# Where the constants load, when the fills go out, and five steps in another order

## The chip, the core and the metric

The kernel runs on one core of a Trainium2 chip. The metric is the device time of one execution in microseconds; lower is better. Before the change the median of three timed runs is 674.17 us (673.79 to 674.68). The core's engines are TensorE (PE; its weight loads are listed as PEld), VectorE (DVE), ScalarE (ACT), GpSimd (POOL) and SyncE (SP, which here only issues DMAs). Each engine runs its own list of instructions in order and waits on semaphores for the others. DMAs are issued by SP, ACT and POOL and are carried out by 16 DMA engines that all queues share.

## The reference

The input is 4096 tokens of 128 values. The six steps of a "macaron" block follow one another, each with a layer norm ahead of it and a residual around it:

```python
x = x + 0.5 * ffn0(norm(x))   # 8 experts 128->512->128, gelu, each token to its argmax expert
x = x + attn0(norm(x))        # grouped causal conv (4 taps), pooled q/k by cumulative sums, gelu MLP
x = x + 0.5 * ffn0(norm(x))   # the same weights as the first
x = x + 0.5 * ffn1(norm(x))   # 16 experts, capacity 320 rows each, relu, softmax gate
x = x + attn1(norm(x))        # s = a*s + W_b u along time, W_c, layer norm
x = x + 0.5 * ffn1(norm(x))   # the same weights as the fourth
```

In `ffn0` every token is computed by one expert out of 8. In `ffn1` a token that comes after the first 320 of its expert is left as it is. All values are float32.

## The kernel before, in words

The tokens lie as 32 tiles of 128 rows in the on-chip array `X`, handled as 8 chunks of four tiles. The stages follow each other: expert pass 0 (`ffn0`), attention, expert pass 1 (`ffn0` again), the first MoE stage (`ffn1`), recurrence, the second MoE stage.

**Expert passes.** A router scores the chunks (`pturn`, `pcopy`, `pscore`), picks the expert (`plog`, `oh`), ranks the tokens (`ra`, `rrank`, `rb`) and computes a row index for each token (`rsel`). POOL then sends each tile of 128 rows to its places in a DRAM table `xs0` with an indirect DMA (`send`, L1620). This is done in groups: pass 0 has two groups of 3 and 5 chunks, pass 1 three groups. The table is then worked through in 84 tiles of one expert each: tiles 0 to 40 belong to pass 0, 41 to 83 to pass 1. For tile i, SP loads its rows (`tload`, L696) and its expert's first weights, 256 KB (`tw`, L703, a ring of four buffers, so a load waits for `tup` of tile i-4); DVE adds the second bias to a copy (`txb`, L1242) and normalises (`tn`, L1233); PE transposes (`tturn`, L817), DVE copies (`tx`, L1247), PE multiplies (`tup`, L827), ACT applies gelu (`tgelu`, L1513), PE multiplies again (`tdown`, L835), DVE joins the residual (`ty`, L1253) and POOL sends the rows back to a DRAM array `y` (`home`, L1624). SP reads `y` back into `X` (`yload`, L711). `txb` reads the row array `RW` after ACT has scaled a part of it (`hb2`, L1484).

**MoE stages.** The second router works by chunk: PE transposes and scores (`pturn`, `pscore` L784), DVE picks an expert (`q1`, seven operations, L1200 to L1214), PE ranks (`qrank`, L809 to L811), DVE makes the row index (`q3`, L1220 and L1227), POOL sends the four tiles (`send`) into a table `xs1` with a place for 320 rows for each of 16 experts. For expert i SP loads rows (`eload`, L730) and weights, 512 KB (`wload`, L722, seven buffers); PE runs `eturn`, `eup` (L900), `edown` (L907), `eback` (L914); DVE makes `eout` (L1387), POOL sends home (L1624).

**Fills.** The tables must hold a neutral row wherever no token is sent. `fill0` writes the places of one group of `xs0` from a zero tile (`ZB`, L633 and L636). `fill1` writes the 320 rows of four experts of `xs1` from `ZX` (four DMAs of 185 KB, L650). The fills of pass 1's three groups are the steps fill.0 to fill.2 of SP's list, those of the first MoE stage's table fill.3 to fill.6, those of the second's fill.7 to fill.10. `FILL_AFTER` (L89) says which semaphore each waits for: `aout` n means that attention chunk n has ended, `edown` n that expert n has.

**Bulk constants.** ACT issues, as its step bulk.1 (L1465 and L1466), two DMAs: the rest of `RW` (256 KB) and all matrices of the attention and recurrence, `MT` (1096 KB), and the semaphore `cm` counts them. Readers are cen.1 on PE (L764), whose result ACT copies in cenc.1; wc.0 on DVE (L998 to L1004); and the attention.

**Recurrence.** For each chunk DVE takes statistics (`rstat`, L1397 and L1401), ACT a square root (`rstd`, L1579), DVE a reciprocal (`rinv`, L1406), ACT normalises (`rnorm`, L1591). ACT's list begins rstd.0, rstd.1, rnorm.0, rnorm.1.

**Order.** The order of all steps on each engine is written out by hand in `TABLE`, one list for each engine; `ORDER` splits it, and the engine programs walk it. A step that waits holds up everything behind it in its own list. Among PE's steps are fillers: `heat` (L920) and `warm` (L932), matmuls of constants into a free bank, whose results nobody reads; each is held back by a semaphore named in `HEAT` or `WARM`. `issued` there counts POOL's sends in the MoE stages.

Of the kernel before, what the change touches and what calls it, by code (L numbers as in the profile page):

```python
# [193 lines left out]
eload.11 eload.12 wload.12 wload.13 wload.14 eload.13 eload.14 eload.15 fill.7 fill.8 wload.15 wload.16 wload.17 fill.9 wload.18 fill.10 yload.16
yload.17 yload.18 yload.19 yload.20 yload.21 yload.22 wload.19 store.0 yload.23 wload.20 wload.21 wload.22 eload.16 eload.17 eload.18 eload.19
eload.20 eload.21 store.1 store.2 store.3 store.4 store.5 store.6 store.7 wload.23 wload.24 eload.22 eload.23 eload.24 wload.25 wload.26 eload.25
eload.26 wload.27 wload.28 eload.27 eload.28 wload.29 eload.29 eload.30 eload.31 wload.30 wload.31""",
# [6 lines left out]
tturn.23 tup.21 tup.22 tturn.24 tdown.20 tdown.21 tdown.22 tturn.25 tup.23 tturn.26 tup.24 tup.25 tdown.23 tdown.24 tup.26 tturn.27 tdown.25 tturn.28
tup.27 tdown.26 tturn.29 tup.28 aturn1.0 aturn1.1 tturn.30 tup.29 tdown.27 aconv.0 tturn.31 tdown.28 tdown.29 aconv.1 tturn.32 tup.30 tturn.33 tup.31
aturn2.0 tup.32 tdown.30 tturn.34 tdown.31 aq.0 tdown.32 tturn.35 ak.0 aturn2.1 tup.33 tup.34 aq.1 av.0 tdown.33 tturn.36 tup.35 ak.1 tup.36 tdown.34
tdown.35 tturn.37 aturn3.0 av.1 tturn.38 tup.37 tup.38 tturn.39 tdown.36 tdown.37 tdown.38 tturn.40 tup.39 aturn3.1 tup.40 aturn4.0 tdown.39 tdown.40
# [4 lines left out]
ak.7 pturn.8 pturn.9 pscore.11 pscore.12 av.7 aup.24 aup.25 aup.26 aturn3.7 aup.27 rrank.3 adown.5 adown.6 aturn4.7 pturn.10 pturn.11 aup.28 aup.29
aup.30 tturn.41 aup.31 tturn.42 tup.41 tturn.43 adown.7 pscore.13 pscore.14 tturn.44 pturn.12 tup.42 tturn.45 tdown.41 tup.43 tturn.46 pscore.15
tup.44 tdown.42 tturn.47 tdown.43 tdown.44 rrank.4 tup.45 tup.46 tup.47 tturn.48 tdown.45 tdown.46 tdown.47 tturn.49 tturn.50 tup.48 tturn.51 tup.49
tup.50 tdown.48 tdown.49 tturn.52 tdown.50 tup.51 tturn.53 tup.52 tup.53 tturn.54 tdown.51 tdown.52 tdown.53 tturn.55 tup.54 tturn.56 tup.55 tup.56
tturn.57 tdown.54 tdown.55 tturn.58 tdown.56 tturn.59 tup.57 tup.58 tturn.60 tturn.61 tup.59 tdown.57 tdown.58 tdown.59 tturn.62 tup.60 tup.61 tup.62
tdown.60 tturn.63 tdown.61 tup.63 tturn.64 tdown.62 tturn.65 tup.64 tdown.63 tturn.66 tup.65 tdown.64 tturn.67 tup.66 tturn.68 tdown.65 tup.67
tdown.66 tturn.69 tup.68 tdown.67 tturn.70 tup.69 tturn.71 tdown.68 tturn.72 tup.70 tup.71 tturn.73 tdown.69 tdown.70 tdown.71 tturn.74 tup.72 tup.73
tup.74 tturn.75 tdown.72 tdown.73 tturn.76 tup.75 tup.76 tturn.77 tdown.74 tdown.75 pturn.13 tturn.78 tup.77 tdown.76 pscore.16 tup.78 tdown.77
qrank.0 tturn.79 pturn.14 pturn.15 tturn.80 pscore.17 tdown.78 tup.79 tup.80 tturn.81 qrank.1 pturn.16 pscore.18 pscore.19 tup.81 tdown.79 tdown.80  # L220
tdown.81 tturn.82 qrank.2 tturn.83 tup.82 tup.83 pturn.17 tdown.82 tdown.83 pscore.20 qrank.3 qrank.4 warm.0 pturn.18 pturn.19 pscore.21 pturn.20
pscore.22 warm.1 warm.2 pscore.23 qrank.5 warm.3 warm.4 qrank.6 qrank.7 warm.5 warm.6 warm.7 warm.8 warm.9 warm.10 warm.11 warm.12 warm.13 warm.14
warm.15 warm.16 warm.17 warm.18 warm.19 warm.20 warm.21 warm.22 warm.23 warm.24 warm.25 warm.26 warm.27 warm.28 eturn.0 eup.0 eup.1 eturn.1 eup.2
# [1535 lines left out]
```

How the kernel before makes its waits and increments, by code:

```python
    def wait_ge(self, sem, value):  # L388
        if self.passed.get(sem.name, 0) < value:
            self.passed[sem.name] = value
            self.eng.wait_ge(sem, value)
# [160 lines left out]
        def wait_r(lane, b):  # L552
            lane.wait_ge(*((sem("pinv"), b + 1) if b < NBS else (sem("ppow"), b - NBS + 1)))
# [32 lines left out]
        def wait_x(lane, k):  # L587
            p, c = divmod(k, NC)
            if p == 0:
                lane.wait_ge(sem(f"y{c}"), 16)
            elif p == 1:
                lane.wait_ge(sem("aout"), c + 1)
            elif p == 2:
                wait_y(lane, NC + c)
            else:
                lane.wait_ge(sem("rout"), c + 1)
# [1 line left out]
        def wait_y(lane, j):  # L598
            lane.wait_ge(sem(f"y{j % NC}"), turns(j + NC, NC))
# [8 lines left out]
        def wait_home(lane, t):  # L609
            lane.wait_ge(sem(f"home{t % NHS}"), turns(t, NHS))
# [6 lines left out]
        def wait_table(lane, g, i):  # L617
            if not IS_LAST[g] or i >= E0:
                lane.wait_ge(sem("rte"), 3 * (g + 1))
# [1 line left out]
        def wait_scattered(lane, g):  # L622
            k = g - GP.index(GP[g])
            lane.wait_ge(sem(f"sent{k}"), 16 * sum(GNT[j] for j in range(g + 1) if j - GP.index(GP[j]) == k))
# [20 lines left out]
        def fill1(e, m, a):  # L645
            SP.wait_ge(sem("zero"), 5)
            for q in range(4 * a, 4 * a + 4):
                dst = xs1[m][q * REACH:q * REACH + CAP, :].rearrange("(p r) d -> p r d", r=5)
                e.dma_start(dst, ZX[0:CAP // 5, :].unsqueeze(1).broadcast_to([CAP // 5, 5, ROWX])).then_inc(sem("fillx"), 16)
```

## Time and profile before

| | |
|---|---|
| timed runs | 674.17 us median, 673.79 to 674.68 |
| profiled execution | 672.23 us, of which 670.8 us from the first instruction to the last |
| mean granted TensorE clock | 0.949 of full speed |
| busy share | PE 92%, DVE 67%, POOL 55%, ACT 48% |
| DMA | 94.19 MB, mean 140 GB/s |
| stages, us from the start | router 0 to 43, expert pass 0 to about 153, attention to 271, expert pass 1 (beginning inside it) to 369, router to 411, first MoE stage to 504, recurrence to 557, second MoE stage to the end |

A row of the timeline gives the start, the duration, the engine, the line and operation, the tiles written and read, and in brackets how long the engine stood idle before it and what ended that wait. The chain of waits is followed back from the last instruction: at each step to what released it. Waits of an engine that is off that chain cost nothing by themselves.

### The profile page before, as it was taken

The numbers are of one execution on the slowest core, as the hardware profiler recorded it, in microseconds if no ns is written. First come the engines' busy times: TensorE is split into PE (matmuls) and PEld (weight loads), VectorE is DVE, ScalarE is ACT, GpSimd is POOL, SyncE is SP. The second block draws the span as 40 slices with busy tenths as digits, with TensorE's granted clock in tenths as the row PEclk, the third lists the DMA queues.
The fourth block names the chain that finished last, engine by engine and source line by source line (L and its number), as shares of the span: only waits on it lengthen the run. The fifth ranks groups of instructions, "written<-read, shape, count | busy, mean of one in ns | idle before, by whom it ended". The sixth has DMA issues, their size and how long they took to land.

```text
span 670.8 us, 13130 instructions
## 1 busy us (share of the span) xinstructions
...
## 2 busy tenths in 40 slices
...
GB/s 266 311 212 194 187 213 202 105 49 201 54 0 83 10 91 61 267 211 201 211 272 99 178 68 104 81 151 141 133 217 142 148 56 51 154 132 142 99 104 15
DMA packets 87031, 94.19 MB, mean 140 GB/s; under 512 B 12156, under 2 KB 65439, under 8 KB 86704
## 3 DMA queue, kind: packets, MB, share of 16 engines
...
q14 instruction: 40, 0.33, 0.2%
...
## 4 chain that ended last, share of the span: by engine, by line
PE 63%; DVE 10%; DMA 8%; POOL 6%; issue 5%; ACT 3%; SPq 3%; ACTq 0%; DVEq 0%
PE ps L835 10%; PE ps L827 10%; PE ps L907 6%; PE ps L900 6%; PE ps L882 4%; PE ps L932 4%; PE ps L784 4%; PE ps L745 4%; POOL y L1624 3%; PE ps L849 3%; PE ps L875 3%; POOL xs L1620 2%; PE ps L945 2%; PE ps L817 2%; DMA X<-y 1%
## 5 line engine op out<-in xcount | busy, mean ns | idle before, releaser
L1620 POOL DMA_INDIRECT xs<-X,IDX x128 | 125.8, 982 | 102.9 <-issue 64.1
L1513 ACT ACTIVATE ht<-ps,CL 128x128 f32<-128x128 f32 x336 | 93.0, 379 | 84.6 <-PE ps L827 84.4
L1624 POOL DMA_INDIRECT y<-yt,xi x84 | 83.1, 989 | 48.9 <-DVE yt L1253 33.5
L827 PE MATMUL ps<-xt,w1s 128*128 128x128 f32 x672 | 86.3, 277 | 1.8 <-DVE xt L1247 0.8
L835 PE MATMUL ps<-W,ht 128*128 (+1 forms) x672 | 85.0, 277 | 2.1 <-ACT ht L1513 1.9
L835 PEld LDWEIGHTS ps<-W,ht 128*128 128x128 f32 x672 | 80.0, 192 | 4.4 <-issue 4.2
L827 PEld LDWEIGHTS ps<-xt,w1s 128*128 128x128 f32 x672 | 80.0, 192 | 3.8 <-DVE xt L1247 2.4
L1611 POOL TENSOR_TENSOR sma<-sma,MH 128x4 f32<-128x4 f32 (+1 forms) x24 | 30.6, 1278 | 71.4 <-DVE sma L962 65.1
L932 PE MATMUL ps<-MT,KC 128*128 128x512 f32 x118 | 58.2, 648 | 1.6 <-DVE IDX L1227 1.2
L1570 ACT ACTIVATE hb<-ps 128x320 f32<-128x320 f32 x64 | 26.7, 428 | 51.1 <-PE ps L900 50.8
L1563 ACT ACTIVATE w1s<-x,SE 128x128 f32<-128x128 f32 (+1 forms) x66 | 27.4, 483 | 43.7 <-DVE SE L1356 43.6
L1611 POOL TENSOR_TENSOR SE<-SE,MH 128x3 f32<-128x3 f32 x32 | 27.9, 873 | 33.7 <-DVE SE L1352 33.5
L1253 DVE SCALAR_TENSOR_TENSOR yt<-ps,xb 128x128 f32<-128x128 f32 x84 | 24.0, 286 | 33.2 <-PE ps L835 32.6
L932 PEld LDWEIGHTS ps<-MT,KC 128*128 128x128 f32 x118 | 23.6, 208 | 29.7 <-issue 21.3
L1624 POOL DMA_INDIRECT y<-xu,x x36 | 34.7, 963 | 16.8 <-DVE xu L1387 8.5
L900 PE MATMUL ps<-ht,W 128*128 128x320 f32 x136 | 41.7, 435 | 0.0
L900 PE MATMUL ps<-ht,wx 128*128 128x320 f32 x120 | 37.3, 436 | 3.4 <-DMA wx<-in_w1x 1.8
L907 PE MATMUL ps<-hb,W 128*128 128x320 f32 x136 | 39.7, 436 | 0.4 <-DVE hb L1374 0.3
L1247 DVE COPY xt<-ps 128x128 f32<-128x128 f32 x84 | 24.2, 288 | 22.1 <-PE ps L817 21.6
L1495 ACT ACTIVATE pxt<-ps 128x512 f32<-128x512 f32 x29 | 16.8, 596 | 40.5 <-PE ps L745 40.3
L1374 DVE TENSOR_SCALAR hb<-ps 128x320 f32<-128x320 f32 x64 | 30.5, 484 | 8.5 <-PE ps L900 8.0
L907 PE MATMUL ps<-hb,wx 128*128 128x320 f32 x120 | 35.1, 435 | 0.4 <-DVE hb L1374 0.3
...
## 6 DMA issues: line engine op xcount, KB each, us to landing
w1s<-in_w SPq DMA_DIRECT2D x84, 256.0 KB
...
X<-y SPq DMA_DIRECT2D x24, 256.0 KB, 4.7
...
```

What stands on the lines that cost most here:

```text
L745: r = e.transpose(dst[:, j * P:(j + 1) * P], src[:, j, 0:P], ident)
L827: r = e.matmul(ps[TILE_BANKS[i % n]][:, c * P:(c + 1) * P], W1[i % NW1][:, c * P:(c + 1) * P], XTT[i % NX][:, :], start=True, stop=True)
L835: r = e.matmul(ps[TILE_BANKS[i % len(TILE_BANKS)]][:, 0:P], HT[i % NHT][:, c, :], W02[:, bass.ds(r0 * F + c * P, P)], start=(c == 0), stop ...
L900: e.matmul(ps[2 + c][:, 0:CAP], WE[k % NW][:, c * P:(c + 1) * P], XET[k % NXET], start=True, stop=True).then_inc(sem("eup"), 1)
L907: r = e.matmul(ps[6 + i % 2][:, 0:CAP], WE[i % NW][:, F + c * P:F + (c + 1) * P], HB[i % 2][:, c, 0:CAP], start=(c == 0), stop=(c == 3))
L932: e.matmul(b[:, F - w:F], ident, MT[:, 0:w], start=True, stop=True)
L1374: e.tensor_scalar(HB[k % 2][:, c, 0:CAP], ps[2 + c][:, 0:CAP], 0.0, None, ALU.max).then_inc(sem("erelv"), 1)
L1513: r = e.activation(HT[i % NHT][:, c, :], ps[TILE_BANKS[i % len(TILE_BANKS)]][:, c * P:(c + 1) * P], ACT.Gelu, bias=CL[:, bass.ds(r0 * 4 + ...
L1563: r = e.activation(EN[i % NEN][0:n, b, :], xe[0:n, b, 0:P], ACT.Identity, scale=se(i, 27)[0:n, b:b + 1], bias=se(i, 30)[0:n, b:b + 1])
L1611: return e.tensor_tensor(dst, src, MH[:, 0:dst.shape[1]], ALU.pow)
L1620: return e.indirect_dma_start(dst, bass.IndirectOffsetOnAxis(ap=IDX[:, n:n + 1], axis=0), X[:, n, 0:w], None, bounds_check=hi, oob_is_err= ...
L1624: return e.indirect_dma_start(dst, bass.IndirectOffsetOnAxis(ap=ix, axis=0), src, None, bounds_check=hi_home, oob_is_err=False, engine_sem ...
```

## The change

Five things are changed. (1) bulk.1 leaves its place ahead of hb2.0 in ACT's list and stands behind tgelu.3, the gelu of the fourth tile; cen.1 (PE), cenc.1 (ACT) and wc.0 (DVE), which need its data, move back too. (2) `FILL_AFTER` is changed: the three fills of pass 1 wait for the first attention chunk, the eight expert fills for the second (four) and the third (four); in SP's list all eleven stand in a row ahead of tw.41, where fill.5 stood one step and fill.6 seven loads further on, and fill.7 to fill.10 behind the last expert load (eload.15) of the first MoE stage. (3) On DVE tn.0 stands ahead of txb.0, q3.5 ahead of q1.7, and rinv.0 ahead of rstat.1. (4) The fillers warm.1 and warm.2 are no longer in PE's list. (5) Nothing else: all instructions but the two fillers are the same. The lists are written here as pieces, since the lines of the table are broken anew:

```diff
-FILL_AFTER = [("aout", 1 + n // 2) for n in range(len(FILL_GROUPS))] + [("aout", n) for n in (3, 3, 4, 4)] + [("edown", n) for n in (2, 4, 6, 8)]
+FILL_AFTER = [("aout", 1) for n in FILL_GROUPS] + [("aout", n) for n in (2, 2, 2, 2, 3, 3, 3, 3)]
 sp:
-fill.3 fill.4 tw.41 fill.5 tload.41
+fill.3 fill.4 fill.5 fill.6 fill.7 fill.8 fill.9 fill.10 tw.41 tload.41
...
-tw.46 tw.47 fill.6 tload.52
+tw.46 tw.47 tload.52
...
-eload.14 eload.15 fill.7 fill.8 wload.15 wload.16 wload.17 fill.9 wload.18 fill.10 yload.16
+eload.14 eload.15 wload.15 wload.16 wload.17 wload.18 yload.16
 pe:
-tdown.6 tdown.7 cen.1 tturn.9
+tdown.6 tdown.7 tturn.9
...
-tup.15 tdown.14 tturn.17
+tup.15 tdown.14 cen.1 tturn.17
...
-pscore.22 warm.1 warm.2 pscore.23 qrank.5 warm.3 warm.4 qrank.6 qrank.7
+pscore.22 pscore.23 qrank.5 warm.3 warm.4 qrank.6 qrank.7
 dve:
-rb.1 rsel.1 txb.0 tn.0 tn.1
+rb.1 rsel.1 tn.0 txb.0 tn.1
...
-txb.9 tn.10 wc.0 ty.6
+txb.9 tn.10 ty.6
...
-tx.17 txb.17 tx.18
+tx.17 txb.17 wc.0 tx.18
...
-q1.5 q1.6 q1.7 q3.5 q3.6 q3.7
+q1.5 q1.6 q3.5 q1.7 q3.6 q3.7
...
-rstat.0 rstat.1 rinv.0 rstat.2
+rstat.0 rinv.0 rstat.1 rstat.2
 act:
-pstd.2 table.1 bulk.1 hb2.0 tgelu.0 tgelu.1 tgelu.2 tgelu.3 tgelu.4
+pstd.2 table.1 hb2.0 tgelu.0 tgelu.1 tgelu.2 tgelu.3 bulk.1 tgelu.4
...
-tgelu.12 cenc.1 tgelu.13
+tgelu.12 tgelu.13
...
-tgelu.17 tgelu.18 tgelu.19
+tgelu.17 tgelu.18 cenc.1 tgelu.19
```

## Rows read from the trace of the kernel before

**Rows 1.** The page's chain of waits, shares of the span by engine.

```profile
PE 63%; DVE 10%; DMA 8%; POOL 6%; issue 5%; ACT 3%; SPq 3%; ACTq 0%; DVEq 0%
```

**Rows 2.** Table by stage: stretch, length, busy time (instructions) per engine, PEclk, DMA share, GB/s.

```profile
44.00:52.00 8.00, 4.76 (x36) 4.26 (x37) 3.26 (x14) 3.31 (x12) 5.82 (x7) 1.00 1.04 366
52.00:60.00 8.00, 6.57 (x54) 6.04 (x55) 2.87 (x11) 2.83 (x11) 6.17 (x7) 1.00 0.46 138
270.00:300.00 30.00, 28.82 (x257) 28.28 (x256) 21.38 (x99) 13.72 (x49) 21.15 (x22) 1.00 0.82 236
366.00:388.00 22.00, 16.78 (x77) 11.70 (x77) 9.56 (x43) 2.98 (x8) 14.76 (x16) 0.69 0.48 150
```

**Rows 3.** Timeline of the first tiles: start, duration, engine, line, operation, [idle before <-releaser].

```profile
43.58 0.33 PE L817 MATMUL ps<-KC,xh 128*128 128x128 f32 x1 [0.45 <-DVE xh L1233]
50.19 0.29 DVE L1242 TENSOR_TENSOR xb<-xi,RW 128x128 f32<-128x128 f32 x1 [3.07 <-DMA xi<-xs]
51.87 1.13 PE L827 MATMUL ps<-xt,w1s 128*128 128x128 f32 x8 [0.55 <-DMA w1s<-in_w]
```

**Rows 4.** Timeline of SP's DMA issues in expert pass 0.

```profile
45.24 1.47 SPq L703 DMA_DIRECT2D w1s<-in_w  x2
59.18 1.16 SPq L696 DMA_DIRECT2D xi<-xs  x2
69.89 0.33 SPq L696 DMA_DIRECT2D xi<-xs  x1
```

**Rows 5.** DMA issues by line: queue, count, KB each, median us to landing.

```profile
X<-y SPq DMA_DIRECT2D x24, 256.0 KB, 4.7
MT<-in_mats ACTq DMA_DIRECT2D x1, 1096.0 KB, 9.0
```

**Rows 6.** Tile loads (xi) from 30 to 110 us, their landing.

```profile
DMA to landing us min/median/max: 2.6/3.2/7.8
```

**Rows 7.** Timeline of DVE in expert pass 0, tiles 10 and 12.

```profile
64.21 0.36 DVE L1233 TENSOR_SCALAR xh<-xi 128x128 f32<-128x128 f32 x1
74.82 0.34 DVE L1233 TENSOR_SCALAR xh<-xi 128x128 f32<-128x128 f32 x1
```

**Rows 8.** Timeline of ACT: the gelu of the fifth tile.

```profile
58.33 1.91 ACT L1513 ACTIVATE ht<-ps,CL 128x128 f32<-128x128 f32 x7 [4.03 <-PE ps L827]
```

**Rows 9.** Timeline of the first dispatch, 381 to 389 us.

```profile
381.23 3.55 PE L932 MATMUL ps<-MT,KC 128*128 128x512 f32 x4
384.62 0.96 PE L784 MATMUL ps<-MBG,pxt 128*128 128x16 f32 x8
388.03 0.97 POOL L1620 DMA_INDIRECT xs<-X,IDX  x1 [2.65 <-DVE IDX L1227]
```

**Rows 10.** Timeline of the end of the first MoE stage, 475 to 500 us.

```profile
475.30 7.64 SPq L650 DMA_DIRECT2D xs<-ZX  x8
482.98 1.69 SPq L722 DMA_DIRECT2D wx<-in_w1x  x2
489.18 0.81 PE L900 MATMUL ps<-ht,wx 128*128 128x320 f32 x2 [1.81 <-DMA wx<-in_w1x]
499.20 0.97 POOL L1624 DMA_INDIRECT y<-xu,x  x1 [0.33 <-DVE xu L1387]
```

**Rows 11.** Timeline of the start of the recurrence.

```profile
508.36 0.84 DVE L1397 BATCH_NORM_STATS2 sma<-X 128x6 f32<-128x128 f32 x4
508.48 0.30 ACT L1579 ACTIVATE sma<-sma,EP 128x4 f32<-128x4 f32 x1 [13.15 <-DVE sma L1401]
509.85 2.60 ACT L1591 ACTIVATE hn<-X,sma 128x128 f32<-128x128 f32 x8
```

**Rows 12.** Timeline of SP between attention and expert pass 1: fills, first weight load.

```profile
208.82 7.51 SPq L650 DMA_DIRECT2D xs<-ZX  x8
238.63 0.36 SPq L703 DMA_DIRECT2D w1s<-in_w  x1
```

**Rows 13.** Table by stage, the stretch of those fills.

```profile
208.80:216.40 7.60, 7.60 (x55) 6.32 (x54) 7.36 (x18) 3.69 (x7) 0.00 (x0) 1.00 0.70 145
```

More of the change, by code:

```diff
@@ L194 @@
[L194 to L197, printed above, removed]
+tw.36 tw.37 tw.38 tw.39 tw.40 yload.3 yload.4 yload.5 yload.6 yload.7 fill.0 fill.1 fill.2 fill.3 fill.4 fill.5 fill.6 fill.7 fill.8 fill.9 fill.10
@@ L204 @@
[L204 to L207, printed above, removed]
@@ L212 @@
[L212 to L215, printed above, removed]
@@ L216 @@
[L216 to L223, printed above, removed]
@@ L240 @@
-edown.31 eback.31""",
+tup.15 tdown.14 cen.1 tturn.17 tup.16 tturn.18 tup.17 tturn.19 tdown.15 tturn.20 tdown.16 tup.18 tup.19 tdown.17 tdown.18 tturn.21 tdown.19 tturn.22
+tup.20 tturn.23 tup.21 tup.22 tturn.24 tdown.20 tdown.21 tdown.22 tturn.25 tup.23 tturn.26 tup.24 tup.25 tdown.23 tdown.24 tup.26 tturn.27 tdown.25
+tturn.28 tup.27 tdown.26 tturn.29 tup.28 aturn1.0 aturn1.1 tturn.30 tup.29 tdown.27 aconv.0 tturn.31 tdown.28 tdown.29 aconv.1 tturn.32 tup.30
+tturn.33 tup.31 aturn2.0 tup.32 tdown.30 tturn.34 tdown.31 aq.0 tdown.32 tturn.35 ak.0 aturn2.1 tup.33 tup.34 aq.1 av.0 tdown.33 tturn.36 tup.35 ak.1
@@ new lines @@
+pscore.8 pscore.9 pscore.10 ak.6 av.6 adown.3 aturn4.4 aturn4.5 aturn3.6 aup.16 aup.17 aup.18 rrank.2 aup.19 aturn2.7 adown.4 aq.7 aup.20 aup.21
+aup.22 aup.23 aturn4.6 ak.7 pturn.8 pturn.9 pscore.11 pscore.12 av.7 aup.24 aup.25 aup.26 aturn3.7 aup.27 rrank.3 adown.5 adown.6 aturn4.7 pturn.10
+pturn.11 aup.28 aup.29 aup.30 tturn.41 aup.31 tturn.42 tup.41 tturn.43 adown.7 pscore.13 pscore.14 tturn.44 pturn.12 tup.42 tturn.45 tdown.41 tup.43
+tturn.46 pscore.15 tup.44 tdown.42 tturn.47 tdown.43 tdown.44 rrank.4 tup.45 tup.46 tup.47 tturn.48 tdown.45 tdown.46 tdown.47 tturn.49 tturn.50
@@ new lines @@
+tdown.71 tturn.74 tup.72 tup.73 tup.74 tturn.75 tdown.72 tdown.73 tturn.76 tup.75 tup.76 tturn.77 tdown.74 tdown.75 pturn.13 tturn.78 tup.77 tdown.76
+pscore.16 tup.78 tdown.77 qrank.0 tturn.79 pturn.14 pturn.15 tturn.80 pscore.17 tdown.78 tup.79 tup.80 tturn.81 qrank.1 pturn.16 pscore.18 pscore.19
+tup.81 tdown.79 tdown.80 tdown.81 tturn.82 qrank.2 tturn.83 tup.82 tup.83 pturn.17 tdown.82 tdown.83 pscore.20 qrank.3 qrank.4 warm.0 pturn.18
+pturn.19 pscore.21 pturn.20 pscore.22 pscore.23 qrank.5 warm.3 warm.4 qrank.6 qrank.7 warm.5 warm.6 warm.7 warm.8 warm.9 warm.10 warm.11 warm.12
@@ L241 @@
+eup.118 eup.119 eback.27 eturn.30 edown.28 eup.120 eup.121 eturn.31 eback.28 edown.29 eup.122 eup.123 eback.29 eup.124 edown.30 eup.125 eup.126
+eup.127 eback.30 edown.31 eback.31""",
     "dve": """
 pstat.0 pstat.1 pstat.2 pinv.0 plog.0 oh.0 pnm.0 ra.0 rb.0 rsel.0 pstat.3 pstat.4 pstat.5 pstat.6 pinv.1 pstat.7 plog.1 pinv.2 plog.2 pnm.1 oh.1 oh.2
[L243 removed]
```

80 lines of the change are left out of this document (43 added, 37 removed).

## The prediction

> **What bounds the kernel now.** I read four views. First the chain of waits [rows 1]: TensorE carries 63% of what ends last, DVE 10%, DMA 8%, POOL 6%. So a microsecond counts only where TensorE stands still for something, or where the sends on POOL are the chain. Second, the table by stage [rows 2] shows where that is: from 44 to 52 us TensorE is busy 4.76 of 8 us while the DMA engines are full (share 1.04); from 366 to 388 it is busy 16.78 of 22 us at a mean granted clock of 0.69. In the attention it has nearly nothing to give. Third, the timeline of each such place, for the instruction that is waited for. Fourth, SyncE's timeline, for what stands ahead of the load that came late. A stage that is bound by TensorE hands a gain made before it on to the stages behind, so the gains add.
>
> **Start of the first expert pass.** Two things hold it.
> First tile: the normalisation tn.0 stands behind txb.0, which waits for ACT's scaling of RW (hb2), and that behind the issue of the bulk constants. Both go. But the fillers on TensorE last until the first transposition: only 0.45 us of idle time stands before it [rows 3], so 0.45 is all this gives.
> Fourth tile: DVE stands 3.07 us until 50.19 for a tile load and TensorE starts tup.3 only at 51.87, on weights that SP issued at 45.24 [rows 3, 4]. In that stretch the constants, 1096 + 256 KB, are on the same engines; the larger takes 9.0 us to land [rows 5]. Without them I take for this 256 KB load the 4.7 us of the other 256 KB loads that SP issues [rows 5]: 49.94, and 0.1 to the matmul, 50.03 instead of 51.87, or 1.85 us. Bounds: 0.45 if it lands as late as now; 2.65 if TensorE's own order is what is left (tup.2 and the transposition before it, 0.45 earlier: about 49.2).
> What is late next: the load of tile 12, issued at 69.89 [rows 4], waits for the last send of group 1. POOL sends those one behind the other and gains only where the first tile's result, 0.45 us earlier at best, stands in its row. Issue 69.89 plus the median landing of 3.2 [rows 6] is 73.1; DVE normalises the tile at 74.82 [rows 7]. So 1.7 us can pass here, and up to 2.1 with what POOL gains; 1.85 does.
> The constants come back: bulk.1 now stands behind tgelu.3, which ends at 58.33 - 4.03 = 54.30 [rows 8], then 1.85 earlier. The issue itself is hidden in ACT's 4.03 us of waiting for TensorE. The transfer lies beside SP's weight loads and the loads of tiles 10 and 11 (issued at 59.18, then about 57.3). Tile 10 is normalised at 64.21 [rows 7], then 62.4: 5 us after its issue. If it takes the 7.8 us of the slowest tile load [rows 6], it lands at 65.1 and 2.7 us are lost, which turns the whole start into 0.85 later than now. At the median it costs nothing. In 52 to 60 the share is 0.46: at the 366 GB/s seen at 1.04 the free half holds some 1.5 MB, more than the 1.35 MB. I take no cost. Term: -1.85, between -2.1 and +0.85.
> The Trainium skill bears on this: "DMA: Bandwidth & Descriptors" (Queues, rings and completion order) says that each DMA engine takes turns, packet by packet, between the queues that have work. By that the loads on SP's queue would keep half the rate beside ACT's constants and be late by under a microsecond; by the slowest row they are late by 4.6. The trace's 3.07 us stand on tile 3 is nearer to the row. The sum would be the same by the rule and 2.7 us higher by the row.
> cen.1, cenc.1 and wc.0 move back with the constants; the same instructions, and their readers (convolution, recurrence, second router) come tens of microseconds later. Zero.
>
> **The fills.** Pass 1's third fill goes out one chunk earlier, and all 32 issues of the expert fills stand ahead of tw.41, at the end of the second and of the third attention chunk. Eight such issues take 7.51 us of SP from 208.82 on [rows 12], so 16 take 15: the last is out at 224. The next on SP, tw.41, is due at 238.63 [rows 12], because it waits for the router; 14.8 us are spare. The eight of now run with a DMA share of 0.70 while TensorE is busy 7.60 of 7.60 us [rows 13]: no slowing is seen, so zero. What leaves the second expert pass (four issues) gives at most the 1.18 us that TensorE is not busy in 270 to 300 [rows 2]; no wait there names these loads, so I take zero.
> In the first MoE stage it is different. At 475.30 SP issues eight fills for 7.64 us, and only then the weights of expert 15, at 482.98; TensorE stands 1.81 us for them until 489.18 [rows 10]. Without the fills that load goes out at 475.3, twelve us ahead of its need at 487.4. What follows is arithmetic: the last rows go home 0.33 us after POOL's last instruction, released by DVE's result and not by a queue of POOL [rows 10]. Term: -1.8, between 0 and -1.81.
>
> **The first dispatch.** POOL stands 2.65 us until 388.03 for q3.5 [rows 9]; its usual gap is 0.30. Ahead of q3.5 stand the two fillers (3.55 us, at half clock) that hold pscore.23 back until 384.62, and then q1.7 on DVE. Both leave. The score matmuls then run at half the clock, twice 0.96 [rows 9], so of about 3.4 us gained some 0.9 goes back: q3.5 is done 2.5 earlier, at 385.3, and earlier still by what q1.7 took. POOL is free at 388.03 - 2.65 = 385.38 and goes on at 385.68. q3.6 is needed only four sends later. 2.35 us go from the chain of sends, on which the loads of the experts wait. I take -2.2, since the 24 fillers that remain ahead of the experts start at a clock that may still be low; between 0 and -2.35.
>
> **The recurrence.** rinv.0 now stands ahead of rstat.1. Today rstat.1 starts at 508.36 with no wait, and ACT's square root for chunk 0 runs from 508.48 for 0.30 [rows 11]. So DVE will stand until 508.8, and rstat.1 begins about 0.6 later. ACT gains nothing from the early rinv.0: rnorm.0 at 509.85 stands behind rstd.1 [rows 11], which needs rstat.1. DVE is nearly full behind it. Between 0 (chunk 1 lands later than now) and +0.6; I take +0.45.
>
> **Sum.** -1.85 - 1.8 - 2.2 + 0.45 = -5.4 on the profiled execution's 672.23, that is 666.8. The median of the timed runs lies 1.94 above that execution; on its scale 674.17 - 5.4 = 668.8 us.
>
> **Rivals.**
> The constants collide where they are now put. For it: the 7.8 us of the slowest tile load, the same 1.35 MB. Against: the share of 0.46 there, and prefetch eight tiles deep. Start term between 0 and +0.85 instead of -1.85: 670.7 to 671.5.
> The dispatch gain ends in another wait: the experts start on fillers or on their weights. For: TensorE is busy with fillers up to the first expert. Against: the loads wait for the sends. 668.8 + 2.2 = 671.0.
> Slower: the clock. Over the 22 us from 366 the granted clock is 0.69, so 13.6 us at the lower level (1.2 GHz); TensorE had stood still, waiting for loads and indices, before it fell. Two fillers leave just this stretch. If TensorE enters the experts at the lower level for as long a spell, 13.6 us of its work double in length for the half that would have been done: 6.8 us, 668.8 + 6.8 = 675.6. It decides from 10.8 us at that level, where it eats the 5.4. Against: 24 fillers, each waiting only for sends that POOL makes in an unbroken row. The Trainium skill's "TensorE: Matmul & The Clock Gate" (HAM oscillation) says that idle gaps put the engine back to half clock until it has been active again; that is what the 0.69 shows.
> The change does not do what it says: the gains are swallowed, because the stage behind starts on something that did not move (POOL's homes, a late landing). About 673.5. Against: the chain's 63% on TensorE.
>
> **How the numbers follow.** The forecast has 0.60 (own range 667.0 to 670.6, from the bounds of its terms); the colliding constants 0.14; the lost dispatch gain 0.09; the swallowed gains 0.10; the clock 0.07. A measurement of this kernel tells about 0.2% (1.35 us) from no change. Faster by more: 0.60 + 0.14 + 0.09 = 0.83; within: 0.10; slower: 0.07. The range that leaves out 0.2: up to the lost gains and halfway to the swallowed ones, 672.3; down to all terms at their best with 1.2 from the second pass (2.1 + 1.81 + 2.35 + 1.18 less 0 = 7.4), 666.7, and half a microsecond for the runs' own spread: 666.2.
>
> **What would show it.** Right: tup.3 near 50 us, no wait of DVE for the fourth tile load; no fill on SP after 225; POOL's sends of the first dispatch 1.28 apart throughout; the weights of expert 15 issued right behind the last expert load and no wait of TensorE for them; DVE standing some 0.35 us ahead of rinv.0. Wrong: a wait of DVE on tile 10 or 11 near 62 us; a granted clock below 1 after the first expert starts; SP late at tw.41; the second pass starting at the time of now.

## The result, and the profile after

| | before | after |
|---|---|---|
| first comparison, 4 executions each | 674.42 us median (673.79 to 677.89) | 665.14 us median (663.77 to 669.42), ratio 0.9874 [0.9832, 0.9915] |
| all later comparisons together | 670.13 us mean, 670.28 median, standard deviation 2.55, 119 executions | 663.74 us mean, 663.63 median, standard deviation 2.12, 21 executions |
| profiled execution (span) | 672.23 (670.8) | 665.63 (663.6) |

The change makes the kernel faster. The first comparison says 9.3 us, the later ones 6.4 us (standard error 0.5; ratio 0.9905 [0.989, 0.992]). Four executions of the kernel before that fell in its slow state (674.9 to 678.1 us) are left out of the second line. The forecast was a gain of 5.4 and a time of 668.8 (666.2 to 672.3); 665.14 lies 1.1 us below that range.

The page of the kernel after, its chain of waits and its clock in 40 slices:

```profile
PE 57%; DVE 12%; POOL 12%; DMA 8%; issue 8%; ACT 3%; SPq 1%; ACTq 0%; DVEq 0%; POOLq 0%
PEclk8599999999999999999998689999999996999999
```

SPq has fallen from 3% to 1% [rows 1], as it would with the fills gone from ahead of expert 15's weights. POOL has doubled to 12%: where TensorE no longer holds the sends up, POOL's own row is the chain. The table by stage, for the stretches of [rows 2] and for one more, 350 to 360:

```profile
44.00:52.00 8.00, 6.93 (x58) 6.28 (x56) 4.06 (x16) 4.45 (x16) 6.10 (x7) 1.00 0.76 213
52.00:60.00 8.00, 6.83 (x56) 6.54 (x57) 3.23 (x14) 2.43 (x9) 5.94 (x7) 1.00 0.92 311
270.00:300.00 30.00, 29.02 (x258) 28.48 (x258) 20.81 (x94) 15.30 (x56) 21.21 (x22) 1.00 0.73 209
350.00:360.00 10.00, 9.73 (x75) 9.49 (x75) 5.90 (x26) 4.35 (x14) 7.74 (x8) 0.84 0.52 153
366.00:388.00 22.00, 17.75 (x76) 12.55 (x77) 10.51 (x47) 2.17 (x5) 16.13 (x17) 0.61 0.51 157
```

From 44 to 52 TensorE is busy 6.93 us instead of 4.76, and the constants' transfer now stands in 52 to 60 (share 0.92 instead of 0.46). The third row has hardly moved. The fourth has a granted clock of 0.84 although TensorE is busy 9.73 of 10 us; this is what the forecast had no place for.

The steps one by one in the kernel after. The start: the fourth tile's matmuls, the constants' two issues, tile 10, the load of tile 12 and tile 12:

```profile
48.69 1.16 PE L827 MATMUL ps<-xt,w1s 128*128 128x128 f32 x8 [0.39 <-DVE xt L1247]
50.67 0.35 ACTq L1465 DMA_DIRECT2D RW<-in_rows  x1
51.05 0.65 ACTq L1466 DMA_DIRECT2D MT<-in_mats  x1
61.26 0.35 DVE L1233 TENSOR_SCALAR xh<-xi 128x128 f32<-128x128 f32 x1
69.09 0.33 SPq L696 DMA_DIRECT2D xi<-xs  x1
72.57 0.40 DVE L1233 TENSOR_SCALAR xh<-xi 128x128 f32<-128x128 f32 x1 [1.08 <-DMA xi<-xs]
```

The fourth tile starts 3.18 us earlier [rows 3]. Tile 10, beside the constants, starts 2.95 earlier and, in this execution, without a wait [rows 7]. Tile 12's load goes out only 0.80 earlier [rows 4], and there DVE now stands 1.08 us: some of the gain goes back. Tile 12 itself is still normalised 2.25 earlier [rows 7].

Other executions with the constants at their new place do wait at tile 10: DVE stands 1.74 us in b_start, 1.56 in a_wide, 0.99 in a_ring11 and 0.37 in a_rinvback (all runs below). In b_start, DVE and then TensorE:

```profile
63.18 0.35 DVE L1233 TENSOR_SCALAR xh<-xi 128x128 f32<-128x128 f32 x1 [1.74 <-DMA xi<-xs]
64.35 0.30 PE L817 MATMUL ps<-KC,xh 128*128 128x128 f32 x1 [0.86 <-DVE xt L1247]
```

That load was issued at 56.34, 6.84 us before the normalisation; in nine executions with the constants at their old place these are 4.9 to 5.1 us, and DVE does not wait.

The timeline further on: SyncE's fills in the attention and the first load behind them; the first send of chunk 5 in the first dispatch; the last weight loads of the first MoE stage and TensorE's matmuls of its last experts (L900, then L907):

```profile
183.90 40.41 SPq L650 DMA_DIRECT2D xs<-ZX  x18
236.14 0.36 SPq L703 DMA_DIRECT2D w1s<-in_w  x1
384.88 0.97 POOL L1620 DMA_INDIRECT xs<-X,IDX  x1 [0.30 <-issue]
473.66 0.90 SPq L722 DMA_DIRECT2D W<-in_w1x  x2
483.39 1.78 PE L900 MATMUL ps<-ht,wx 128*128 128x320 f32 x6
485.33 2.36 PE L907 MATMUL ps<-hb,wx 128*128 128x320 f32 x8
```

And the table by stage beside the fills:

```profile
207.00:224.00 17.00, 17.00 (x99) 12.16 (x98) 16.33 (x58) 7.35 (x14) 5.22 (x4) 1.00 0.72 149
```

The last fill is out at 224.3 and the weight load behind it, which waits for the router, at 236.14, no later than before [rows 12]. TensorE is busy 17.00 of 17 us at full clock beside them, as beside the eight of before [rows 13]. POOL's stand of 2.65 us is the usual 0.30 [rows 9]. TensorE no longer stands for expert 15: the L900 row at 483.39 has no wait [rows 10].

### The profile page after: what moved, and what is told of

Read it like the earlier page. It is cut to its first block, busy times and chain, and to the rows that moved or that the text cites. A ratio compares the mean times of both kernels' runs of the same rounds, so it can differ in the third digit from the quotient of the medians.

```text
span 663.6 us, 13121 instructions
## 1 busy us (share of the span) xinstructions
PE 612.0 (92%) x3647; PEld 472.9 (71%) x3647; DVE 448.8 (68%) x1882; ACT 323.4 (49%) x1037; POOL 367.2 (55%) x377
## 4 chain that ended last, share of the span: by engine, by line
PE 57%; DVE 12%; POOL 12%; DMA 8%; issue 8%; ACT 3%; SPq 1%; ACTq 0%; DVEq 0%; POOLq 0%
PE ps L907 8%; PE ps L900 8%; PE ps L835 8%; PE ps L827 8%; POOL xs L1620 8%; PE ps L932 4%; PE ps L784 3%; PE ps L882 3%; PE ps L745 3%; PE ps L849 3%; POOL y L1624 2%; PE ps L875 2%; DMA y<-yt,xi 2%; PE ps L890 1%; PE ps L914 1%
## 5 line engine op out<-in xcount | busy, mean ns | idle before, releaser
L827 PE MATMUL ps<-xt,w1s 128*128 128x128 f32 x672 | 86.7, 278 | 1.9 <-DVE xt L1247 1.2
L835 PEld LDWEIGHTS ps<-W,ht 128*128 128x128 f32 x672 | 81.4, 195 | 4.3 <-issue 4.2
L827 PEld LDWEIGHTS ps<-xt,w1s 128*128 128x128 f32 x672 | 80.2, 192 | 4.3 <-DVE xt L1247 2.2
L932 PE MATMUL ps<-MT,KC 128*128 128x512 f32 x114 | 55.8, 646 | 0.4
L1624 POOL DMA_INDIRECT y<-xu,x x36 | 34.7, 964 | 14.7 <-issue 8.3
L900 PE MATMUL ps<-ht,W 128*128 128x320 f32 x136 | 41.7, 435 | 0.0
L907 PE MATMUL ps<-hb,W 128*128 128x320 f32 x136 | 39.7, 436 | 0.4 <-DVE hb L1374 0.3
L900 PE MATMUL ps<-ht,wx 128*128 128x320 f32 x120 | 37.1, 435 | 1.6 <-DVE ht L1368 1.3
L907 PE MATMUL ps<-hb,wx 128*128 128x320 f32 x120 | 35.1, 436 | 0.4 <-DVE hb L1374 0.3
```

The lines of the kernel that those rows point to most:

```text
L827: r = e.matmul(ps[TILE_BANKS[i % n]][:, c * P:(c + 1) * P], W1[i % NW1][:, c * P:(c + 1) * P], XTT[i % NX][:, :], start=True, stop=True)
L835: r = e.matmul(ps[TILE_BANKS[i % len(TILE_BANKS)]][:, 0:P], HT[i % NHT][:, c, :], W02[:, bass.ds(r0 * F + c * P, P)], start=(c == 0), stop ...
L900: e.matmul(ps[2 + c][:, 0:CAP], WE[k % NW][:, c * P:(c + 1) * P], XET[k % NXET], start=True, stop=True).then_inc(sem("eup"), 1)
L907: r = e.matmul(ps[6 + i % 2][:, 0:CAP], WE[i % NW][:, F + c * P:F + (c + 1) * P], HB[i % 2][:, c, 0:CAP], start=(c == 0), stop=(c == 3))
L932: e.matmul(b[:, F - w:F], ident, MT[:, 0:w], start=True, stop=True)
L1624: return e.indirect_dma_start(dst, bass.IndirectOffsetOnAxis(ap=ix, axis=0), src, None, bounds_check=hi_home, oob_is_err=False, engine_sem ...
```

## The experiments

Fifteen runs, in the order of the questions. "At equal clock" means: the times of 244 executions of eleven kernels were fitted with one level for each kernel and one slope on the mean granted clock; the slope is -0.40 us (+-0.03) for each 0.001, and levels have a standard error of about 0.55.

### Is 9.3 us the change?

b_same, the kernel before, and a_same and a_again, the kernel after; nothing is edited:

```diff
 (no line differs)
```

> The kernel before, unchanged, once more. Theory A (single spells at the lower clock level come and go between executions of one and the same kernel): the spells that its first profile showed at 224.0 to 227.4 us and at 541.5 to 544.9 us are not both there again, others may stand elsewhere, and the times of its executions differ by 0.66 us for each 0.001 of their mean granted clock. Theory B (each spell belongs to the order of the instructions): the same spells at the same places within 1 us, and the executions agree in clock to 0.001. Time: ratio 1.000 in both.

> The changed kernel, unchanged, once more. Theory A: its single spell at 356.8 to 360.2 us is gone or elsewhere, a spell near 220 or near 537 may be there as in the kernel before, and executions between 663 and 669 us follow their mean granted clock by 0.66 us for each 0.001. Theory B: the same spells again, clock 0.957 in each. Time: ratio 0.987 (0.985 to 0.990) in both.

> The changed kernel again, as the base for the next three and for more executions. Theory A (the change is worth 5.5 to 6.5 us; the 9.3 us of the first comparison hold 3 to 4 us of low spells of the clock that its few executions of the kernel before happened to have): ratio 0.990 to 0.992. Theory B (the change is worth 9.3): ratio 0.986 to 0.987.

Measured: b_same 671.49 us median (664.97 to 675.66), ratio 1.0016 [0.9983, 1.0049]; a_same 661.81 (660.85 to 666.96), 0.9904 [0.9869, 0.9938]; a_again 663.75 (660.80 to 667.80), 0.9912 [0.9884, 0.9939]. One and the same kernel spreads over 10 us. Between 40 and 660 us the clock records show the lower level (1.2 GHz) in these stretches:

```
first execution before: 224.0-227.4  370.8-384.4  387.9-391.3  541.5-544.9  551.7-568.8
b_same                : 368.2-381.8  385.2-388.7  487.6-491.1  538.8-545.7  552.5-569.6
first execution after : 356.8-360.2  370.5-387.5  551.4-561.6
a_same                : 355.7-359.1  369.4-386.5  543.5-560.5
a_again               : 366.8-383.9  547.7-557.9
```

The table by stage, 220 to 230 us, of the kernel before in its first execution and then in b_same:

```profile
220.00:230.00 10.00, 10.00 (x62) 8.20 (x61) 8.64 (x26) 4.52 (x11) 4.21 (x3) 0.83 0.00 1
```

```profile
220.00:230.00 10.00, 10.00 (x72) 8.38 (x72) 9.51 (x28) 5.61 (x14) 3.73 (x3) 1.00 0.00 1
```

Of the same kernel, 62 matmuls are through in one and 72 in the other. Theory A holds: single spells come and go with the execution. So the comparison of the two profiles cannot be read as the change alone: the 1.7 us that the attention seemed to win, the 1.7 us that pass 1 seemed to lose at 357 and the 2.7 us that the second dispatch seemed to win are such spells. The slope came out lower than the 0.66 expected, as it would if part of the low time costs nothing (a_wide below has such a stretch). The 6.4 us lie inside the first comparison's interval (5.7 to 11.3); why its four executions of the kernel before stand 5.0 us above the mean of the later 119 stays open. The later comparisons ran on four chips, where the kernel before has means of 669.2, 669.9, 670.9 and 671.0 us; on which chip the first one ran is not on record, so a difference between chips is not ruled out. The Trainium skill, "TensorE: Matmul & The Clock Gate" (Part 1: The HAM clock gate), says that the moment of the change does not follow the kernel's start and so differs from run to run; the rows above agree. The same page of the Trainium skill puts the ramp at the start of the matmuls at under 1% of a typical span; the spells here lie far behind the start, and executions of one kernel span 1.6% (664.62 to 675.24).

### The four parts, one at a time on the kernel before

b_start and b_disp:

```diff
-act: table.1 bulk.1 hb2.0 ... tgelu.3 tgelu.4
+act: table.1 hb2.0 ... tgelu.3 bulk.1 tgelu.4
-dve: rsel.1 txb.0 tn.0
+dve: rsel.1 tn.0 txb.0
...
-pe: pscore.22 warm.1 warm.2 pscore.23
+pe: pscore.22 pscore.23
-dve: q1.6 q1.7 q3.5
+dve: q1.6 q3.5 q1.7
```

(the first two edits, with cen.1, cenc.1 and wc.0 as in the change, are b_start; the last two are b_disp)

> Only the first part of the change: bulk constants behind the gelu of the fourth tile with their readers further back, normalisation of the first tile ahead of its bias copy. Theory of the trace after (3.1 us won at the fourth tile and 2.1 given back because later tile loads wait for buffers that POOL's row of sends and homes frees): the fourth tile's up matmuls at 48.7 us, gain 0.9 to 1.0 at 110 us, time 673.4 or ratio 0.9986, apart from spells of the clock. My forecast's theory (the gain at tile four stays): gain 1.85, ratio 0.9973. Rival (the start also causes the gains in the attention and the second dispatch): ratio 0.993 or less.

> Only the first dispatch: index of chunk 5 ahead of the pick of chunk 7, two fillers out. Theory of both traces: the 2.65 us that POOL stood before the sends of chunk 5 fall to 0.3, all later sends 2.35 us earlier, and the first expert 2.3 to 2.8 earlier; time 671.9, ratio 0.9965, apart from spells. Rival (gain lost at the experts' start): ratio 1.000, first expert not earlier than 1 us.

b_fills and b_rinv:

```diff
-FILL_AFTER = ... [("aout", 1 + n // 2) ...] + [("aout", n) for n in (3, 3, 4, 4)] + [("edown", n) for n in (2, 4, 6, 8)]
+FILL_AFTER = ... [("aout", 1) ...] + [("aout", n) for n in (2, 2, 2, 2, 3, 3, 3, 3)]
...
-dve: rstat.0 rstat.1 rinv.0 rstat.2
+dve: rstat.0 rinv.0 rstat.1 rstat.2
```

> Only the fills of both expert tables moved into the attention. Theory of the traces: the weights of expert 15 are issued right behind the last expert load, TensorE's 1.81 us of standing before 489 go, and with them the low spell of the clock that followed that stand in one execution of the kernel before (487.6 to 491.1, another 1.7 us in the executions that have it): gain 1.8 to 2.6, ratio 0.9961 to 0.9973; nothing lost in the attention, SP on time at tw.41. Rival (16 fills in a row slow the attention): chunk 3 or 4 of the attention later by 1 us or more, ratio 0.999 or above. Rival (the fills explain all that the other parts leave of the change's gain of 5.5): gain 3 or more, ratio 0.9955 or less.

> Only the reciprocal of the recurrence's chunk 0 ahead of the statistics of chunk 1. My forecast: chunk 1's statistics 0.5 to 0.6 later, 0.3 to 0.45 lost, ratio 1.0005, which the times cannot tell from 1. Rival (it is this that brings the 2.6 us won in the second dispatch): ratio 0.996, and both spells of low clock at 541 and from 552 to 569 shorter.

| part | ratio | against the kernel before | at equal clock | by stage in the traces |
|---|---|---|---|---|
| b_start | 1.0019 [0.9982, 1.0056] | -0.1 +-0.9 | -1.0 | -0.8 |
| b_disp | 1.0002 [0.9967, 1.0036] | -1.0 +-0.8 | -2.2 | -2.5 |
| b_fills | 0.9977 [0.9952, 1.0001] | -1.9 +-0.6 | -3.1 | -3.0 |
| b_rinv | 1.0007 [0.9979, 1.0036] | +0.6 +-0.8 | +0.3 | +0.2 |
| sum | | -2.4 | -6.0 | -6.0 |
| whole change | 0.9905 | -6.4 +-0.5 | -6.0 | |

No part alone can be told from nothing by its times: each interval holds 1 (the fills' just so), because the spells' spread is as large as the part. Two readings go further. At equal clock the parts add up to the whole. This takes it that a part does not itself change the clock, which is not shown: the three parts that gain ran at a mean clock of 0.951, the kernel before at 0.954, each 1.5 to 2.5 standard errors lower. In b_wide below, where the edit does change the clock, the same fit turns 1.8 us won into 2.4 lost. Without it the four parts sum to -2.4 +-1.7. So the weight lies on the traces: the last column takes the time between two instructions on either side of the edit, as a mean over all profiled executions with and without that part. The second L1132 is DVE's step of `rsel` that makes the row indices of pass 0's second group; the x copy is `tx`.

```
from -> to                                     without the part        with it         executions
second L1132 -> x copy of tile 27         64.50 (64.00 to 65.12)  63.71 (62.74 to 64.23)   6 / 6
last send of chunk 4 -> first of chunk 5   3.80 (3.62 to 4.07)     1.28 (all)              5 / 6
statistics of expert 11 -> eout of 15     41.51 (40.57 to 43.12)  38.55 (38.54 to 38.56)   6 / 6
first rstat -> first rout                 14.14 (13.93 to 14.43)  14.38 (all)              7 / 5
```

(a_ring15, b_ring15, a_ring11, b_narrow4 and b_wide4 below are left out; for the second row b_wide too, where it is 1.93.) The rivals of the parts fall: of the 2.4 us that b_disp's sends come earlier than those of b_same 2.1 are left at the first expert's result, b_fills loses nothing in the attention but a spell, and b_rinv's second dispatch, 41.4 us from its first send to its last, lies among those of kernels without it (40.4 to 44.6).

The third row hides two things. In four executions the time is 40.57 to 41.05, 2.25 us more than with the fills moved; in b_same and b_rinv it is 43.12 and 42.74. TensorE of b_same, at expert 15:

```profile
486.43 0.81 PE L900 MATMUL ps<-ht,wx 128*128 128x320 f32 x2 [2.67 <-DMA wx<-in_w1x]
487.40 4.01 PE L907 MATMUL ps<-hb,wx 128*128 128x320 f32 x8
```

The eight L907 take 4.01 us instead of 2.36: the clock fell right behind the stand, and cost another 1.7 us. That is how the fills come to 3.0 on the mean and not 1.8. With b_narrow4, b_wide4 and b_ring15 such a spell follows the stand in 4 of the 9 executions that have one; in the 8 with the fills moved there is no stand and no spell.

a_rinvback takes the worst part out of the kernel after:

```diff
-rstat.0 rinv.0 rstat.1 rstat.2
+rstat.0 rstat.1 rinv.0 rstat.2
```

> The changed kernel with the reciprocal of the recurrence's chunk 0 back behind the statistics of chunk 1. By the trace (0.30 us lost between the stages' first statistics and the first output) 0.3 us faster than the changed kernel; by the part alone, whose executions came out 0.8 slower at equal clock, up to 0.8 faster. If the reciprocal were what shortens the second dispatch, 1 to 2.6 us slower than the changed kernel.

Measured: 665.25 us median, ratio 0.9924 [0.9889, 0.9959]; against the kernel after +1.6 +-1.0, at equal clock +0.2 +-0.7. The 0.2 us of the stage table can't be seen in the times. It is no better version.

### Why does the clock fall while TensorE is busy?

Ahead of the spell at 224 TensorE of the kernel before runs the router's scores, 24 matmuls of 8 columns back to back. b_narrow4 and b_wide4 add three times as many; the results are read by nobody:

```diff
+for j in [j for n in range(3 if i in (8, 9, 10) else 0) for j in range(CT)]:
+    e.matmul(bk[:, 256:256 + en], XT[i % NXT][:, j, :], w, ...)       # b_narrow4: 8 columns
+    e.matmul(bk[:, 256:256 + P], XT[i % NXT][:, j, :], ident, ...)    # b_wide4 instead: 128 columns
```

> The kernel before with 72 score matmuls of 8 columns added, in free columns of the bank that nobody reads, ahead of the 24 scores of attention chunks 0 to 2 (219 to 222 us): TensorE is busy for 8 us more without a gap. Theory N (the clock falls because these matmuls move few columns, though TensorE reads as busy): a low spell begins inside the stretch, between 221 and 233 us, and lasts past its end; the chunk's end is 8 us and 2 to 5 us more behind. Rival I (only idle time lowers the clock): no spell between 200 and 240, chunk's end 8 us behind.

> The same 72 matmuls more, with the same stationary operands, but with 128 columns moved in each, in free columns of the bank. Theory N: no low spell between 219 and 231 us; one behind the 24 scores of 8 columns may come as in the kernel before. Rival I: no spell in either. Third (length of the stretch or the loads of the stationary operand lower the clock): a spell as with 8 columns.

Table by stage of b_narrow4, then of b_wide4:

```profile
214.00:220.00 6.00, 6.00 (x22) 3.10 (x21) 5.86 (x26) 2.79 (x4) 1.12 (x2) 1.00 0.63 130
220.00:230.00 10.00, 10.00 (x63) 9.98 (x61) 2.99 (x12) 0.89 (x3) 4.10 (x3) 0.67 0.00 0
230.00:240.00 10.00, 10.00 (x39) 8.52 (x39) 1.81 (x6) 1.79 (x5) 0.00 (x0) 0.50 0.00 1
```

```profile
214.00:220.00 6.00, 6.00 (x22) 3.08 (x21) 5.86 (x27) 2.82 (x5) 1.56 (x2) 1.00 0.56 116
220.00:230.00 10.00, 10.00 (x92) 10.00 (x92) 2.56 (x9) 0.62 (x2) 3.67 (x3) 1.00 0.00 0
230.00:240.00 10.00, 10.00 (x63) 7.28 (x63) 9.26 (x28) 6.95 (x16) 0.00 (x0) 1.00 0.00 1
```

Both read as 10.00 of 10 us busy. With 8 columns the clock is low from 223.3 to 240.4, with 128 it is full throughout. From the first score to the attention's next step it takes 17.3 us and 10.6 us, against 2.6 without the added ones: 14.7 and 8.0 more, where 10 to 13 and 8 were expected. The single executions took 687.92 and 673.59 us. Their timelines, one block of each:

```profile
223.71 5.27 PE L785 MATMUL ps<-WRC,pxt 128*128 128x8 f32 x24
```

```profile
223.08 2.92 PE L785 MATMUL ps<-KC,pxt 128*128 128x128 f32 x24
```

At full clock the first block of 8 columns takes 2.74 us and one of 128 takes 2.84 to 2.92: the wider matmul costs 4 to 8 ns more. In these two executions, one of each kernel, rival I and the third reading fail. The Trainium skill's "TensorE: Matmul & The Clock Gate" (HAM oscillation) speaks of idle gaps; b_same at 486 shows such a gap, but the rows here show a fall without one.

So the scores were widened, in both kernels:

```diff
-r = e.matmul(b[:, j * en:(j + 1) * en], XT[...][:, j, :], w, ...)
+r = e.matmul(b[:, j * en:(j + m) * en].rearrange("p (m e) -> p m e", e=en), XT[...][:, j, :],
+             w.unsqueeze(1).broadcast_to([P, m, en]), ...)              # m = 128 // en from pass 1 on
```

> The kernel before with the scores of 128 columns alone. Theory N: no low spell near 224 and 541 us, executions 1 to 3.4 us faster than the kernel before on the mean, ratio 0.995 to 0.9985, mean granted clock 0.958 or more against 0.954. Rival: as the kernel before.

> The changed kernel, but all router scores from the second pass on move 128 columns (the 8 or 16 of the router repeated, of which the first copy is read). By the run with 72 added score matmuls each costs 4 ns more, 0.1 us for 24. Theory N (few moved columns let the clock fall while TensorE is busy): no low spell between 40 and 365 us, none near 541, that is 1 to 3.4 us less than the changed kernel on the mean and a smaller spread of the executions; the spells in the two dispatches, where TensorE stands still, stay. Rival (these spells have another cause): a spell between 200 and 365 us or near 537 is still there, time as the changed kernel.

Measured: b_wide 668.48 us median, ratio 0.9963 [0.9931, 0.9994], mean granted clock 0.964 against 0.954; a_wide 664.14, ratio 0.9909 [0.9878, 0.9940], clock 0.966 against 0.955. Neither has a spell near 224, 357 or 541; b_wide has one at 310.0, so not all come from scores. One profile each says little, since those of a_again and b_disp have none there either; the clocks of all executions say more: 0.961 to 0.966 in the 12 of b_wide (0.942 to 0.962 in the kernel before) and 0.964 to 0.969 in the 12 of a_wide (0.947 to 0.960 in the kernel after). The spell in the first dispatch was expected to stay and shrank too, to 6.8 us, in both; the prediction had put the 0.69 there to TensorE's standing alone. Table by stage, first dispatch, of a_again and then of a_wide:

```profile
366.00:388.00 22.00, 18.80 (x68) 12.21 (x69) 8.83 (x41) 1.79 (x3) 16.66 (x18) 0.61 0.52 164
```

```profile
366.00:388.00 22.00, 16.68 (x74) 10.92 (x73) 9.66 (x45) 1.79 (x3) 16.63 (x18) 0.84 0.52 160
```

The clock is 0.84 instead of 0.61, and POOL is busy 16.63 and 16.66 us: the chain there is its row of sends, 1.28 apart in both. So the kernel before gains 1.8 +-0.7 us, and the kernel after nothing (+0.7 +-0.8): I expected 1 to 3.4 of it. In the first dispatch the reason can be read: from the last send of chunk 4 to the first of chunk 5 b_wide takes 1.93 us instead of 3.80, and in the kernel after the change had already taken that stand away (1.28). Why the spells that are gone near 357 and 541 win the kernel after nothing stays open. Nothing here beats the kernel after.

### Where the start's gain goes

a_ring15, b_ring15 and a_ring11 change the number of buffers for tile rows (NXI) and results (NYT):

```diff
-NXI, NXH, NX, NW1, NHT, NYT, NXB = 13, 3, 3, 4, 4, 14, 4
+NXI, NXH, NX, NW1, NHT, NYT, NXB = 15, 3, 3, 4, 4, 15, 4     # the rings of a_ring15, b_ring15
+NXI, NXH, NX, NW1, NHT, NYT, NXB = 11, 3, 3, 4, 4, 14, 4     # a_ring11
```

> The changed kernel with 15 buffers instead of 13 for tile rows and 15 instead of 14 for results. Theory H (of the 2.5 us won at the fourth tile 1.6 are given back in tiles 9 to 27, because SyncE's tile loads wait 1.9 to 3.5 us for POOL to send tiles home): that wait of SyncE falls below 0.5, tile 27 is 0.5 to 1.2 us earlier against the first router than in the changed kernel (63.5 us there on the mean), time 0.5 to 1.2 us less. Rival S (given back at tile 12 already, whose load waits for the last send of the second group): the wait for homes goes, but tile 27 is as late as now within 0.3. Rival P (TensorE's own work bounds these tiles): as S.

> The kernel before with the same 15 and 15 buffers. Theory H: its tile loads hardly wait for homes (no such wait in its traces from 60 to 110 us), so nothing is won: ratio 1.000, tile 27 as before within 0.3 (64.5 us after the first router).

> The changed kernel with 11 buffers for tile rows, two fewer. Theory H: tile loads wait for homes two sends (2 x 1.28 us) longer, SyncE's wait for them from 60 to 110 us above 5 us, tile 27 later by 1.5 to 2.6 us. Rivals S and P: tile 27 later by less than 0.5.

SyncE's waits from 60 to 110 us (line, what it waited for, us in all, times, longest), of the kernel after, then of a_ring15. L688 waits for sends, L391 for homes:

```profile
SPq L703 <- PE ps L827: 7.6, 8, 2.8
SPq L688 <- DMA xs<-X,IDX: 3.8, 1, 3.8
SPq L391 <- DMA y<-yt,xi: 3.5, 3, 1.9
SPq L696 <- DVE xh L1233: 0.3, 1, 0.3
```

```profile
SPq L703 <- PE ps L827: 11.8, 8, 3.2
SPq L688 <- DMA xs<-X,IDX: 2.5, 1, 2.5
```

The wait for homes is gone, as H said, but no time came of it: 666.16 us median, ratio 0.9929 [0.9896, 0.9961], against 0.9912 and 0.9904 of the kernel after. Its tile 27 stands 64.57 us behind the second L1132, against 63.7. In this execution the clock was low until 40.9 us, the fillers ahead of the first tile ended late (first transposition at 45.08), and so the lead to be given back was small (0.9 us at tile 8, 1.8 to 2.8 in the others); all of it went, but not where H has it: it is still 0.9 at tile 16. b_ring15: 670.86, 1.0005 [0.9968, 1.0043], no gain, as expected; its tile 27 stands at 65.17, in an execution of 677.33 us, where 64.5 within 0.3 was expected. In a_ring11 tile 27 is 4.8 us later (68.55), but its wait for homes is 2.5 us, not above 5; the table by stage says what happened:

```profile
70.00:76.00 6.00, 3.53 (x25) 2.77 (x24) 1.22 (x4) 1.63 (x6) 4.58 (x5) 1.00 0.56 136
76.00:84.00 8.00, 6.29 (x29) 5.99 (x30) 3.00 (x12) 1.81 (x8) 5.28 (x6) 0.57 0.76 212
```

TensorE stood 2.5 of 6 us, the clock fell, and the next 8 us ran at 0.57; how much of the 4.8 us is the clock's was not taken apart. So: in this one execution fewer buffers hurt, more do not help, and the wait for homes is not what limits the kernel after. Rival S (tile 12 behind the last send) covers only a part, as the lead at the copies of x shows (six executions without b_start's part less six with it, us):

```
tile    3     8    12    14    16    18    20    27
lead  2.5   2.5   2.2   1.8   1.7   1.0   0.9   0.8
```

At tiles 12 to 14, where DVE waits for tile loads, 0.6 to 0.7 go. The largest step, at tile 18, has nothing to do with buffers: it is where cen.1 and wc.0 now stand. Kernel after, TensorE with cen.1 and the transposition of tile 19, and DVE with the first and the last operation of wc.0; then the transposition of tile 19 in the kernel before:

```profile
81.28 0.41 PE L764 MATMUL ps<-MT,KC 128*128 128x144 f32 x2
84.13 0.33 PE L817 MATMUL ps<-KC,xh 128*128 128x128 f32 x1 [0.44 <-DVE xh L1233]
82.24 0.28 DVE L998 TENSOR_REDUCE CM<-MT 128x1 f32<-128x128 f32 x1
83.06 0.31 DVE L1004 TENSOR_TENSOR MC<-MC,RW 128x128 f32<-128x128 f32 x1
```

```profile
85.75 0.27 PE L817 MATMUL ps<-KC,xh 128*128 128x128 f32 x1
```

TensorE is busy without a gap there until it waits for tile 19, which DVE normalises only behind wc.0. From the first matmul (L827) of tile 15 to that of tile 16, with cen.1 between them, it takes 2.14 us in all eight executions with the part and 1.90 in all nine without; from tile 17 to tile 18, with wc.0, 3.29 to 3.56 and 2.90 to 3.02. In a_ring15 these steps take its lead from 0.9 to 0.65 and 0.25. What cen.1 costs at its new place (0.24) is about what leaves its old one (3.69 to 3.81 us instead of 3.86 to 4.19 from tile 7 to tile 8, where tile 10 is not waited for); for wc.0 no such gain is seen. No run puts wc.0 elsewhere.

## Why the prediction was right or wrong

**What failed.** First, a step of "Sum" and one of "How the numbers follow". The forecast is "on its scale 674.17 - 5.4 = 668.8 us": it hangs on a median of three executions, and the range left "half a microsecond for the runs' own spread". The kernel's own standard deviation is 2.55 us, and 674.17 lies 4.0 above its mean of 670.1. With that mean the same sum gives 664.7, against 663.7 measured. Of the effect itself, 5.4 was forecast against 6.4 +-0.5 (6.0 at equal clock). That these are so near is in part luck: the term of the start is 1.05 us too large and that of the fills 1.2 too small. Term by term:

**Start, -1.85, measured -0.8.** The fourth tile comes 2.5 us earlier on the mean (8.8 instead of 11.3 us behind the second L1132), so the weights' landing was sized too small. Then 1.7 is given back between tiles 8 and 27. The step "1.7 us can pass here, and up to 2.1" held at tile 12, where 2.15 pass on the mean. What failed is that the working stops there, and that it puts the moved readers of the constants at "Zero": 0.35 more goes at tile 14 and about 0.55 at tile 18, where wc.0 now stands ahead of work that TensorE waits for. "I take no cost" for the constants' transfer failed in part too: DVE waits 0.37 us or more for tile 10 in four of the eight executions with the constants there, and in b_start and a_wide 0.7 to 0.9 us of that reach TensorE. The late load of b_start, 6.84 us, is nearer to the prediction's slowest row than to its delay of under a microsecond.

**Fills, -1.8, measured -3.0.** The mechanism is right: 2.25 us without a spell. The term is too small since the clock can fall behind such a stand of TensorE, in 2 of these 6 executions, for 1.7 more. In the attention they cost nothing, as said.

**Dispatch 1, -2.2, measured -2.5.** As worked out. The lower clock does not reach the experts: the low stretch of 17 us ends at 387.5, some 20 us ahead of the first expert's turn at 407.7, and TensorE was on its fillers in between. That was the slower rival's place (0.07).

**Recurrence, +0.45, measured +0.24.** DVE of the kernel after stands ahead of the reciprocal, as said, and the second chunk's statistics start late:

```profile
503.92 0.18 DVE L1406 RECIPROCAL sma<-sma 128x4 f32<-128x4 f32 x1 [0.36 <-ACT sma L1579]
504.01 0.84 DVE L1397 BATCH_NORM_STATS2 sma<-X 128x6 f32<-128x128 f32 x4
```

About half of that delay is taken up ahead of the first output.

**Not in the sum.** Spells of the lower clock in the attention, at the end of pass 1 and in the second dispatch. They move a pair of profiles by 1.7 to 2.7 us in either direction, and were named only as the slower rival, at one place. Of the other rivals, the colliding constants came in part (the wait at tile 10), and the start's gain was swallowed in part; the dispatch gain was not lost.
